# How far the expert stage runs ahead of the attention stage: a fixed lead in the merged order of an attention and expert-layer kernel

## The chip, the cores and the metric

The kernel runs on the 8 cores of one Trainium2 chip. Every core works on one sequence of 4096 tokens and writes its own output; nothing is exchanged between the cores. The metric is the device time of the slowest core in microseconds (us), lower is better.

## What is computed

For each sequence x (4096 tokens, 1024 numbers each) the reference does one linear-attention layer and one mixture-of-experts layer, each between two layer normalizations and with a residual:

```python
# attention: 8 heads of 64
q, k, v = x @ Wq, x @ Wk, x @ Wv
q = softmax(q, axis=-2) * SCALE        # over the 64 numbers of a head
k = softmax(k, axis=-1)                # over the 4096 tokens
context = einsum('bhdn,bhen->bhde', k, v)
out = einsum('bhde,bhdn->bhen', context, q) ... @ Wo + bo
# experts: 16 routed, top 2 by softmax score, and 2 shared
xe = einsum('bsd,eod->bseo', u, Wr) + br
routed = einsum('bse,bseo->bso', g_topk, xe)
shared = (einsum('bsd,eod->bso', u, Ws) + sum(bs)) / N_s
ffn = u + routed + shared
# the layer
x = x + layernorm(attn(layernorm(x)))
x = x + layernorm(ffn(layernorm(x)))
```

## The kernel before

The 4096 tokens are 32 tiles of 128. All 18 expert matrices are applied to every token, and the gate (zero for the experts that were not chosen) multiplies each product as it is added up, so the expert layer is a dense pass of 18 matrices of 1024 by 1024.

First comes a pass over all 32 tiles for keys and values (tags a1_...), which ends with the context. Everything behind it is one list, `flow_tail`. It has six windows, w = 0 to 5, and each merges two lists:

- `la`, the attention items of quarter w (8 tiles, taken in pairs, 21 items a tile, 168 items in all). For a tile: the query product (a2_p_q, L798), its exponential on ScalarE, the softmax division on VectorE (qn, L485 to L494), a transpose on TensorE (trqn, L811), the product with the context (o2, L823) and its copy (L509), the output product (wo, L840), bias and statistics (att, L518 to L526), normalization and residual (y, L530 to L539), the second normalization (ub, L545), its transpose (trub, L852), the scores (sc, L861), the gates on VectorE (g, L564 to L584, a chain of 12 small operations) and their transpose (trg, L870). Windows 4 and 5 have none.
- `lb`, the expert items: for w of 2 and more the final step of quarter w-2 (`fin_quarter`, 24 items: for each of 8 tiles statistics of the sum racc, the normalization L633 and the residual L636, with the residual loaded to yld and the result stored by DMA), then the expert pass of quarter w-1 (`ffn_quarter`, 644 items). That pass starts with s = 0: 16 groups of five matmuls (one of L879 and four of L884), which put the biases and u itself into racc through the copy L605. Then for s = 1 to 18 and both halves oh of the output (36 units) it loads a block of weights two units ahead (ffnl, 8 transposing DMAs, L400 to L404) and runs 8 groups, one a token tile: eight matmuls (ffnp, L895) and one multiply-and-add into racc on VectorE (ffnv, L610).

`prop_merge` (L275) writes the common order of a window: behind each item of `la` it puts items of `lb`, at the rate of `len(lb)/len(la)` times 0.65, so that about a third of `lb` is left over and stands at the window's end without attention items. Every engine takes its own items from the one list in that order, and each queue is executed strictly in order: TensorE (PE), VectorE (DVE), ScalarE (ACT) and the DMA queue of SyncE (SP), which holds all loads and stores of this part.

The products land in six PSUM banks (pb). They are given out while the list is read: each product takes the bank whose last reader stands furthest back in the list, and waits for that reader. The transposes have two banks of their own (pbT). The expert products of a quarter cannot be copied to racc before the final step of the quarter ahead has read racc (the wait at L602 for vFF of the same tile).

On SP a weight load ffnl waits until the unit that used the buffer has ended (L398), and the item a2_v_y (L374) stores the attention result and loads the rows of x and of the normalized input for two tiles later (L377 to L391).

Of the kernel before, what the change touches and what calls it, by code (L numbers as in the profile page):

```python
# [85 lines left out]
def build_nc():  # L86
# [185 lines left out]
        its.append(("finb", q, QT - 1))  # L272
        return its

    def prop_merge(la, lb):  # L275
        outl = []
        na, nb = len(la), len(lb)
        if na == 0:
            return list(lb)
        ratio = nb / na  # L280
        ib = 0
        for ia in range(na):
            outl.append(la[ia])
            want = int(round((ia + 1) * ratio * 0.65))
            while ib < want:
                outl.append(lb[ib]); ib += 1
        outl.extend(lb[ib:])
        return outl
# [4 lines left out]
    for w in range(NQ + 2):  # L293
        la = []
        if w < NQ:
            for t in range(QT * w, QT * w + QT, 2):
                la += zip_merge(a2_items(t), a2_items(t + 1))
        lb = []
        if 2 <= w:
            lb += fin_quarter(w - 2)  # L300
        if 1 <= w <= NQ:
            lb += ffn_quarter(w - 1)
        flow_tail += prop_merge(la, lb)
# [776 lines left out]
```

How the kernel before makes its waits and increments, by code:

```python
    def ms(self, eng, chan, label):  # L61
        self._bump(chan, label, 1)
        if self.mode == "emit":
            eng.drain().then_inc(self.sem[chan], 1)
# [1 line left out]
    def pe_ms(self, instr, chan, label):  # L66
        self._bump(chan, label, 1)
        if self.mode == "emit":
            instr.then_inc(self.sem[chan], 1)
# [1 line left out]
    def op_ms(self, instr, chan, label):  # L71
        self._bump(chan, label, 1)
        if self.mode == "emit":
            instr.then_inc(self.sem[chan], 1)
# [1 line left out]
    def dma(self, eng, chan, label, out, in_, **kw):  # L76
        self._bump(chan, label, 16)
        if self.mode == "emit":
            eng.dma_start(out=out, in_=in_, **kw).then_inc(self.sem[chan], 16)
# [1 line left out]
    def wait(self, eng, chan, label):  # L81
        if self.mode == "emit":
            eng.wait_ge(self.sem[chan], self.vals[chan][label])
```

## Times and profile before

| | us |
|---|---|
| time, median of 2 runs | 3333.73 (3290.99 and 3376.48) |
| profiled execution, its own time | 3106.46 |
| its span (slowest core, core 1) | 3104.8 |
| spans of the 8 cores | 3079.2 to 3104.8 |
| PE matmul busy | 2449.4 (79%) |
| DVE busy | 1578.0 (51%) |
| ACT busy | 113.7 (4%) |

The profiled execution is one run of the program; its own time stands below both timed runs. A row of the timeline shows when an instruction or a merged run of equal ones starts, how long it lasts, the engine and line, the operation and, in brackets, how long the engine had been idle before it and what ended that. "DVEq" is the queue of VectorE, that is a semaphore that VectorE sets when its work has drained.

### The profile page before, as it was taken

To read this page: it belongs to the slowest core of one execution; us is meant where nothing else is said; L and a number is where in the kernel's file an instruction comes from. 1 tells how busy PE (TensorE), PEld (TensorE's weight loads), DVE (VectorE), ACT (ScalarE), POOL (GpSimd) and SP (SyncE) were. 2 spreads that over 40 slices of the span, in tenths; PEclk is the share of its full clock that TensorE was granted. 3 is DMA by queue.
4 is the path that set the end of the run, shared out by engine and by line. 5 is a ranking of instruction groups with operands and counts; after the bars stand their busy time and mean duration, and the time that the engine had idled before them with its cause. 6 is when DMAs were issued, how large, how long until landed. Compare 5 with 4: busy or idle time off the path is not lost.

```text
span 3104.8 us, 38462 instructions; the slowest of 8 cores (3079.2 to 3104.8 us)
## 1 busy us (share of the span) xinstructions
PE 2449.4 (79%) x12014; PEld 1109.0 (36%) x12014; DVE 1578.0 (51%) x2882; ACT 113.7 (4%) x353; POOL 15.8 (1%) x29
## 2 busy tenths in 40 slices
PE   3243350349999999499999994999999949999994
PEld 1121120114444444234444442444444414444442
DVE  4132332666656644566566445666564454444445
ACT  0000000000000000000000000000000000000000
POOL 0000000000000000000000000000000000000000
PEclk9666675669999999799999996999999979999997
DMA  5989889213334433424344334243434342333334
GB/s 109 136 123 131 153 125 136 80 60 75 72 87 101 102 76 75 142 77 96 67 102 102 78 75 144 74 98 66 101 82 80 75 143 55 80 75 77 78 75 133
DMA packets 678005, 296.33 MB, mean 95 GB/s; under 512 B 632337, under 2 KB 643089, under 8 KB 676660
## 3 DMA queue, kind: packets, MB, share of 16 engines
q1 hardware_dynamic: 672628, 251.86, 34.0%
q0 software_dynamic: 5184, 42.01, 11.9%
q8 instruction: 107, 1.75, 0.2%
q14 instruction: 86, 0.70, 0.1%
HBM read 142.78 MB, written 79.69 MB: 72 GB/s over the span
## 4 chain that ended last, share of the span: by engine, by line
PE 65%; DVE 11%; DMA 7%; DVEq 6%; issue 4%; another core or an unknown queue 3%; SPq 3%; ACT 0%; POOL 0%; ACTq 0%; POOLq 0%
PE pb L895 56%; DMA xA<-xin 6%; SPq L79 2%; DVEq L424 2%; PE pb L840 2%; PE pb L798 2%; PE pb L884 2%; DVE att L535 1%; DVEq L64 1%; DVE ftmp L636 1%; DMA cen_st<-cen 1%; DVEq L532 1%; PE pb L754 1%; DVE Dbn L422 1%
## 5 line engine op out<-in xcount | busy, mean ns | idle before, releaser
L895 PE MATMUL pb<-wrt,uT 128*128 128x512 bf16 x9216 | 2019.7, 380 | 1.1 <-issue 0.3
L895 PEld LDWEIGHTS pb<-wrt,uT 128*128 128x128 bf16 x9216 | 895.5, 98 | 1072.7 <-issue 11.2
L610 DVE SCALAR_TENSOR_TENSOR racc<-pb,gAll,racc 128x512 f32<-128x512 f32 x1024 | 758.4, 750 | 836.1 <-PE pb L895 811.3
L740 PE MATMUL pbT<-eye,hb 128*128 128x128 bf16 x256 | 32.1, 306 | 236.0 <-DVEq L64 235.6
L610 DVE SCALAR_TENSOR_TENSOR racc<-pb,halfc,racc 128x512 f32<-128x512 f32 x128 | 96.1, 751 | 124.9 <-PE pb L895 124.9
L852 PE MATMUL pbT<-eye,ub 128*128 128x128 bf16 x256 | 23.1, 243 | 138.0 <-DVEq L64 137.7
L740 PEld LDWEIGHTS pbT<-eye,hb 128*128 128x128 bf16 x256 | 24.8, 138 | 242.1 <-issue 241.9
L422 DVE BATCH_NORM_STATS2 Abn<-xA 128x6 f32<-128x512 f32 x32 | 22.2, 693 | 154.2 <-DMA xA<-xin 150.8
L461 DVE CAST vb<-pb 128x512 bf16<-128x512 f32 x32 | 22.2, 694 | 107.9 <-PE pb L767 82.9
L884 PE MATMUL pb<-eyeblk,uT 128*128 128x512 bf16 x256 | 77.0, 430 | 0.0
L811 PE MATMUL pbT<-eye,qn 128*128 128x128 bf16 x128 | 13.5, 233 | 78.6 <-DVEq L64 78.2
L852 PEld LDWEIGHTS pbT<-eye,ub 128*128 128x128 bf16 x256 | 18.4, 109 | 149.1 <-issue 146.5
L535 DVE TENSOR_TENSOR att<-att,xA 128x1024 f32<-128x1024 f32 x32 | 39.2, 1226 | 62.0 <-DMA xA<-xin 55.5
L840 PE MATMUL pb<-wob,o2b 128*128 128x512 bf16 x256 | 66.6, 410 | 1.9 <-DVEq L64 1.9
L754 PE MATMUL pb<-wkb,hT 128*128 128x512 bf16 x256 | 67.8, 431 | 0.0
L798 PE MATMUL pb<-wqb,hT 128*128 128x512 bf16 x240 | 62.7, 413 | 0.4 <-issue 0.2
L605 DVE COPY racc<-pb 128x512 f32<-128x512 f32 x64 | 42.5, 689 | 33.8 <-PE pb L884 29.3
L879 PE MATMUL pb<-brx,gTx 18*128 18x512 bf16 x64 | 27.4, 429 | 40.1 <-DVE racc L605 40.1
L767 PE MATMUL pb<-wvb,hT 128*128 128x512 bf16 x256 | 56.6, 379 | 0.0
L721 ACT ACTIVATE Elv<-Eag,epsc 128x1 f32<-128x1 f32 x32 | 9.5, 297 | 1283.5 <-DVEq L64 1283.5
L494 DVE TENSOR_SCALAR qn<-qe,rq 128x64 bf16<-128x64 f32 x256 | 44.7, 250 | 4.6 <-issue 2.0
L633 DVE TENSOR_SCALAR ftmp<-racc,Eag,Ers 128x1024 f32<-128x1024 f32 x32 | 26.0, 812 | 41.0 <-DMA yld<-yscr 32.2
(109 smaller groups left out, 908.4 us busy)
## 6 DMA issues: line engine op xcount, KB each, us to landing
xA<-xin SPq DMA_DIRECT2D x128, 256.0 KB, 5.8
wbf<-wr POOLq DMA_DIRECT2D x16, 2048.0 KB, 39.8
wrt<-wbf SPq DMA_TRANSPOSE x1152, 2.8
yscr<-att SPq DMA_DIRECT2D x32, 512.0 KB, 3.5
yld<-yscr SPq DMA_DIRECT2D x32, 512.0 KB, 4.2
out<-ftmp SPq DMA_DIRECT2D x32, 512.0 KB, 2.9
hscr<-hT SPq DMA_DIRECT2D x32, 256.0 KB, 41.3
hT<-hscr SPq DMA_DIRECT2D x60, 128.0 KB, 4.6
```

Of the source, the lines that this page charges most:

```text
L79: eng.dma_start(out=out, in_=in_, **kw).then_inc(self.sem[chan], 16)
L422: v.bn_stats(bn[:, 0:6], src[:, 0:512])
L424: v.drain()
L535: v.tensor_tensor(att[i][:], att[i][:], xA[i][:], ALU.add)
L610: ii = v.scalar_tensor_tensor(rsl, pb[bk][:], gcol, rsl, ALU.mult, ALU.add)
L740: last = pe.transpose(pT[:, kk * P:(kk + 1) * P], hb4[i4][:, kk * P:(kk + 1) * P], eye[:])
L754: last = pe.matmul(pb[0 if i == 0 else 4][:], hT4[i4][:, kk * P:(kk + 1) * P], wkb[:, kk * HID:(kk + 1) * HID], start=(kk == 0), stop=(kk ...
L767: last = pe.matmul(pb[1 if i == 0 else 5][:], hT4[i4][:, kk * P:(kk + 1) * P], wvb[:, kk * HID:(kk + 1) * HID], start=(kk == 0), stop=(kk ...
L798: last = pe.matmul(pb[bk][:], hsrc[:, kk * P:(kk + 1) * P], wqb[:, kk * HID:(kk + 1) * HID], start=(kk == 0), stop=(kk == 7))
L840: last = pe.matmul(pb[bk][:], o2b[i][:, jx * P:(jx + 1) * P], wob[:, jx * D + oh * HID:jx * D + (oh + 1) * HID], start=(jx == 0), stop=(jx ...
L884: last = pe.matmul(pb[bk][:], uT[:, kk * NTOK + tt * P:kk * NTOK + (tt + 1) * P], eyeblk[:, kx * HID:(kx + 1) * HID], start=False, stop=(k ...
L895: last = pe.matmul(pb[bk][:], uT[:, kk * NTOK + tt * P:kk * NTOK + (tt + 1) * P], wrt[par][:, kk * HID:(kk + 1) * HID], start=(kk == 0), s ...
```

## The change

`prop_merge` gets a parameter `lead` with the value 36. The first 36 items of `lb` are now put ahead of the first item of `la`, and the rest of `lb` is spread by its own rate, `(len(lb) - 36)/len(la)` times 0.65. Window 0 has no `lb`, and windows 4 and 5 no `la`, so that their lists stay as they were. In window 1 (`lb` of 644) the 36 items are the 32 of s = 0, one weight load, one full group and the product of the next. In windows 2 and 3 (`lb` of 668) they are the 24 items of the final step and 6 groups of s = 0. The rate behind them goes from 2.49 to 2.35 items of `lb` for an attention item in window 1, and from 2.58 to 2.45 in windows 2 and 3.

```diff
-    def prop_merge(la, lb):
+    def prop_merge(la, lb, lead=36):
         outl = []
         na, nb = len(la), len(lb)
         if na == 0:
             return list(lb)
-        ratio = nb / na
-        ib = 0
+        lead0 = min(lead, nb)
+        ib = lead0
+        outl.extend(lb[:ib])
+        ratio = (nb - lead0) / na
         for ia in range(na):
             outl.append(la[ia])
-            want = int(round((ia + 1) * ratio * 0.65))
+            want = min(nb, lead0 + int(round((ia + 1) * ratio * 0.65)))
             while ib < want:
                 outl.append(lb[ib]); ib += 1
         outl.extend(lb[ib:])
```

The changed file is two lines longer, so its line numbers behind this place are higher by 2: L895 there is L897.

**Place 1: TensorE at the start of window 2.** Before, the two query products (L798) come first, then the two transposes of qn (L811), and only then the first groups of s = 0 (L879 and L884) with the products of the context (L823) between them:

```order
L895 MATMUL pb<-wrt,uT 128x512 x912
L798 MATMUL pb<-wqb,hT 128x512 x16
L811 MATMUL pbT<-eye,qn 128x128 x8
L879 MATMUL pb<-brx,gTx 128x512
L884 MATMUL pb<-eyeblk,uT 128x512 x4
L823 MATMUL pb<-qTt,ctx 64x128 x8
```

Now six groups of s = 0 stand ahead of the first query product; these rows are the sixth of them and what follows:

```order
L881 MATMUL pb<-brx,gTx 128x512
L886 MATMUL pb<-eyeblk,uT 128x512 x4
L800 MATMUL pb<-wqb,hT 128x512 x8
L881 MATMUL pb<-brx,gTx 128x512
L886 MATMUL pb<-eyeblk,uT 128x512 x4
L800 MATMUL pb<-wqb,hT 128x512 x8
```

The query products moved behind six groups, and eight groups now stand between the first query product and the first transpose of qn.

**Place 2: VectorE at the start of window 2.** Before, the softmax division of the first two tiles (L485, L489, L494) stands inside the final step (statistics L422 to L425, results L633 and L636):

```order
L422 BN_STATS Ebn<-racc 128x6
L423 BN_STATS Ebn<-racc 128x6
L425 BN_AGGR Eag<-Ebn 128x2
L485 TENSOR_REDUCE qs<-qe 128x8
L489 RECIPROCAL rq<-qs 128x8
L494 TENSOR_SCALAR qn<-qe,rq 128x64 x8
L633 TENSOR_SCALAR ftmp_58<-racc,Eag,Ers 128x1024
L636 TENSOR_TENSOR ftmp_58<-ftmp_58,yld_56 128x1024
```

Now the final step runs through, and the division stands behind eleven copies of s = 0 (L607):

```order
L635 TENSOR_SCALAR ftmp_59<-racc,Eag,Ers 128x1024
L638 TENSOR_TENSOR ftmp_59<-ftmp_59,yld_57 128x1024
L607 COPY racc<-pb 128x512 x11
L487 TENSOR_REDUCE qs<-qe 128x8
L491 RECIPROCAL rq<-qs 128x8
L496 TENSOR_SCALAR qn<-qe,rq 128x64 x8
L607 COPY racc<-pb 128x512
```

The attention work left the final step; the final step is now as it always was in window 4.

**Place 3: TensorE in window 1, the last pair of tiles.** Before, 104 matmuls (13 groups) of the expert pass stand between the second output product (L840) and the first transpose of ub (L852):

```order
L840 MATMUL pb<-wob,o2b 128x512 x8
L895 MATMUL pb<-wrt,uT 128x512 x104
L852 MATMUL pbT<-eye,ub 128x128 x8
L895 MATMUL pb<-wrt,uT 128x512 x8
L852 MATMUL pbT<-eye,ub 128x128 x8
```

Now it is 96 (12 groups), and at the pair's end the two transposes of the gates have no group between them (x2):

```order
L842 MATMUL pb<-wob,o2b 128x512 x8
L897 MATMUL pb<-wrt,uT 128x512 x96
L854 MATMUL pbT<-eye,ub 128x128 x8
L897 MATMUL pb<-wrt,uT 128x512 x8
L854 MATMUL pbT<-eye,ub 128x128 x8
L897 MATMUL pb<-wrt,uT 128x512 x32
L863 MATMUL pb<-ct_bf,uT 128x16 x8
L897 MATMUL pb<-wrt,uT 128x512 x8
L863 MATMUL pb<-ct_bf,uT 128x16 x8
L897 MATMUL pb<-wrt,uT 128x512 x64
L872 MATMUL pbT<-eye,gb 16x128 x2
```

One group moved out of the stretch to the window's end. Over the four pairs this stretch had 14, 12, 13 and 13 groups in window 1 and has 13, 12, 12 and 12; in windows 2 and 3 it had 13, 13, 13 and 14 each and has 13 four times.

## Rows read from the trace of the kernel before

**Rows 1.** Page: busy tenths of PE and its granted clock in 40 slices.
```profile
PE   3243350349999999499999994999999949999994
PEclk9666675669999999799999996999999979999997
```
**Rows 2.** Waits of PE from 680 us: total us, times, longest us.
```profile
PE pbT L811 <- DVEq L64: 60.1, 6, 22.1
PE pb L879 <- DVE racc L605: 40.1, 1, 40.1
PE pbT L852 <- DVEq L64: 28.3, 13, 3.9
PE pb L823 <- DVEq L64: 21.8, 2, 11.1
PE pbT L870 <- DVEq L64: 12.9, 13, 1.8
```
**Rows 3.** Timeline of PE, start of window 2.
```profile
1224.67 43.33 PE L895 MATMUL pb<-wrt,uT 128*128 128x512 bf16 x200
1267.84 3.62 PE L798 MATMUL pb<-wqb,hT 128*128 128x512 bf16 x16
1293.36 0.59 PE L811 MATMUL pbT<-eye,qn 128*128 128x128 bf16 x4 [21.91 <-DVEq L64]
...
1320.05 0.60 PE L879 MATMUL pb<-brx,gTx 18*128 18x512 bf16 x1
...
1322.40 0.38 PE L879 MATMUL pb<-brx,gTx 18*128 18x512 bf16 x1
```
**Rows 4.** Timeline of PE, start of window 4.
```profile
2505.42 0.38 PE L879 MATMUL pb<-brx,gTx 18*128 18x512 bf16 x1
...
2553.33 0.58 PE L879 MATMUL pb<-brx,gTx 18*128 18x512 bf16 x1 [40.13 <-DVE racc L605]
...
2558.02 0.38 PE L879 MATMUL pb<-brx,gTx 18*128 18x512 bf16 x1
...
2559.30 0.39 PE L879 MATMUL pb<-brx,gTx 18*128 18x512 bf16 x1
```
**Rows 5.** Timeline of VectorE, final step in window 2.
```profile
1282.15 0.81 DVE L633 TENSOR_SCALAR ftmp<-racc,Eag,Ers 128x1024 f32<-128x1024 f32 x1 [9.68 <-DMA yld<-yscr]
...
1319.55 1.89 DVE L605 COPY racc<-pb 128x512 f32<-128x512 f32 x3 [0.26 <-DVEq L64]
```
**Rows 6.** Timeline of VectorE, final step in window 4.
```profile
2521.53 0.81 DVE L633 TENSOR_SCALAR ftmp<-racc,Eag,Ers 128x1024 f32<-128x1024 f32 x1 [11.22 <-DMA yld<-yscr]
...
2552.50 3.68 DVE L605 COPY racc<-pb 128x512 f32<-128x512 f32 x6 [0.26 <-DVEq L64]
```
**Rows 7.** Timeline of PE, window 1: gaps ahead of three kinds of transposes.
```profile
699.18 0.38 PE L811 MATMUL pbT<-eye,qn 128*128 128x128 bf16 x4 [1.96 <-DVEq L64]
...
799.24 0.38 PE L811 MATMUL pbT<-eye,qn 128*128 128x128 bf16 x4 [1.29 <-DVEq L64]
...
845.91 1.01 PE L852 MATMUL pbT<-eye,ub 128*128 128x128 bf16 x8 [3.94 <-DVEq L64]
...
948.75 0.61 PE L852 MATMUL pbT<-eye,ub 128*128 128x128 bf16 x8 [2.26 <-DVEq L64]
```
**Rows 8.** Timeline of PE, last pair of window 2.
```profile
1661.02 0.61 PE L852 MATMUL pbT<-eye,ub 128*128 128x128 bf16 x8 [1.09 <-DVEq L64]
```
**Rows 9.** Timeline of VectorE, window 1 ahead of ub of the second pair.
```profile
831.02 2.07 DVE L610 SCALAR_TENSOR_TENSOR racc<-pb,gAll,racc 128x512 f32<-128x512 f32 x3 [0.26 <-issue]
...
842.18 2.73 DVE L610 SCALAR_TENSOR_TENSOR racc<-pb,gAll,racc 128x512 f32<-128x512 f32 x4 [0.26 <-PE pb L895]
```
**Rows 10.** Timeline of SP's DMA queue, window 1, first pair.
```profile
728.23 24.04 SPq L79 DMA_TRANSPOSE wrt<-wbf  x16
...
757.32 1.21 SPq L79 DMA_DIRECT2D hT<-hscr  x2
```
**Rows 11.** Page: time from issue to landing (last number) of the loads of hT.
```profile
hT<-hscr SPq DMA_DIRECT2D x60, 128.0 KB, 4.6
```

## The prediction

> **What bounds the kernel now.** I read the page's slices first. From the tenth slice on TensorE is at nine tenths or more, apart from a dip at each of the slices 17, 25 and 33 and at the end, and in those dips the granted clock falls to about 0.6 or 0.7 [rows 1]. So behind the first two windows (where nothing changes) the time is TensorE's own work plus its gaps. That work is the same before and after: the change only reorders. A group of the expert pass (eight matmuls of 512 columns) takes 1.73 us: 25 groups fill 1224.67 to 1267.84 [rows 3].
>
> The waits of TensorE from 680 us say which gaps exist [rows 2]. All end at VectorE: transposes of qn (L811) 60.1 us in 6 waits, the context product (L823) 21.8 in 2, transposes of ub (L852) 28.3 in 13, transposes of the gates (L870) 12.9 in 13, and one wait of 40.1 us of the s = 0 groups (L879). That is 163 us. The timeline of TensorE splits them. The long ones are the starts of windows 2, 3 and 4, where the final step of a quarter keeps VectorE; the short ones recur in each pair of attention tiles. The window starts are what a lead could help, and the short gaps are what a lower rate of expert groups could harm.
>
> **Window starts, before.** In window 2 the last expert group ends at 1267.84 and TensorE is back in steady work at 1320.05 [rows 3], 52.2 us. Inside it did the two query products (2 x 1.73, as they are eight such matmuls each), two transposes and two context products (some 1.2 together at full clock, my estimate from a duration of 0.6 at the low clock for the transposes [rows 3], halved) and three groups of s = 0. A group of s = 0 takes 1.28 at full clock, 2558.02 to 2559.30 [rows 4]. So 8.5 us of the 52.2 were work and 43.7 were lost. The next group still runs at the low clock, 2.35 instead of 1.28 [rows 3], which makes 44.8.
>
> **Window starts, after.** Six groups of s = 0 come first. They fill the six banks, and the query product behind them needs a bank whose copy VectorE makes only after the final step. So the lead does not put TensorE 18 groups ahead here: it goes six groups and stops. This is exactly what window 4 does already: its seventh group waits 40.1 us [rows 4]. What remains is when VectorE gets through. Residual rows land 14.3 us after the last group (1267.84 to 1282.15 [rows 3, 5]), behind the last weight loads on SP's queue, which the change leaves where they are. From there to the first copy the final step takes 31.0 us when it runs through, 2521.53 to 2552.50 [rows 6]; with the attention items between it took 37.4, 1282.15 to 1319.55 [rows 5]. TensorE resumes 0.8 after the first copy starts [rows 4, 6]. 14.3 + 31.0 + 0.8 = 46.1, less six groups of work (7.7) is 38.4 lost. The clock is low afterwards: the first two groups take 4.7 (2553.33 to 2558.02) for 2.6 of work [rows 4], 2.1 more. That is 40.5 against 44.8: **4.3 us less in each of windows 2 and 3, 8.6 together.** If the residual rows land as in window 4 (16.1 after the last group, 2505.42 to 2521.53 [rows 4, 6]) it is 2.5 each, 5.0 together.
>
> Here the Trainium skill speaks against the change: Perfetto Trace Analysis, section Optimization Strategy, says that where a kernel has several regimes with different busiest engines, interleaving them may improve it, and the lead takes the attention items out of the final step. The trace has both forms, and the interleaved one is not better here, since both regimes want VectorE (37.4 us against 31.0 [rows 5, 6]). By the rule the sum's first term would be a loss; what it would cost is in the second rival.
>
> **What leaves the final step's cover.** The softmax divisions of the first pair (half of 37.4 - 31.0, some 3 us a tile) now stand behind the final step, between groups of s = 0. Window 1 had this arrangement before, and TensorE waited 1.96 us for the second transpose of qn [rows 7]. I charge the same to windows 2 and 3, 3.9, and take off 0.7 in window 1, whose first pair now stands among the longer expert groups as its second pair does, with a gap of 1.29 [rows 7]. **3.2 us more.** Its bounds are 0 (VectorE catches up during ten groups) and 12.8 (all 6.4 us exposed twice).
>
> **The lower rate.** Between the second output product and the first transpose of ub, VectorE runs without a pause (bias, statistics, residual, statistics, ub) and TensorE arrives first. The gap follows the number of expert groups in that stretch: 14 groups 1.09 [rows 8], 13 groups 2.26, 12 groups 3.94 [rows 7]. So a group less costs 1.2 to 1.7 there. VectorE's side gives the same from below: its add takes 0.69 when it is busy (three in 2.07, four in 2.73 [rows 9]), and 1.73 - 0.69 = 1.04. The order has three groups fewer in window 1 (14, 12, 13, 13 before, 13, 12, 12, 12 after) and one fewer in each of windows 2 and 3. Five groups at 1.25 are **6.2 us more**; bounds 5.2 and 8.5. The gates' transposes wait about 1 us a pair (12.9 in 13 [rows 2]), for the second tile's chain mostly; their group counts stay near what they were, but the last pair of window 1 loses the one group between its two transposes: **1 us more**, between 0 and 1.7.
>
> **Edits that cost nothing.** In window 1 the 16 groups of s = 0 move ahead of the query products. They need what is there, and TensorE does the same work. The weight loads keep their place relative to the expert groups that need them. The stores and loads of a2_v_y move past weight loads on SP. Before, in window 1, 16 of these took 24.0 us and the last hT load went out at 757.32 + 1.21 [rows 10]; with 4.6 to land [rows 11] it was there at 763, and no wait for hT stands among TensorE's waits [rows 2]. After, the shortest way from the end of the awaited unit to the query product is 17 groups, 29.4 us, against 12 us for its eight weight loads, some 6 for the two tiles' own transfers and 4.6 to land, 22.6. It stays covered by 7 us.
>
> **The sum.** -8.6 + 3.2 + 6.2 + 1.0 = +1.8 us. On the profiled execution (3106.5, of which 3104.8 is span) that is 3108. The median of the two timed runs is 3333.7, 227 us above the profiled execution of the same program, for which these rows have no cause. The terms are in VectorE's and TensorE's durations, so I add them as they are: 3335.5, written as 3336.
>
> **Rivals.**
> (1) The lead helps more than I charge. Speaking for it: the attention items now come when expert groups are there to cover them, and a VectorE that is less behind might also shorten the gaps inside pairs. Against: these gaps follow the group counts, and the counts fall. If all short gaps of the pairs went (28.3 + 12.9 + 3.3) with the 8.6, that would be -53 us: 3053 on the profiled scale, 1.7% faster. A third of it is already generous.
> (2) The lost interleave costs, slower. The place is the first pair of windows 2 and 3, and then every pair's stretch ahead of ub. If the 6.4 us of attention work on VectorE are exposed in both windows (12.8), the residual lands late enough to take the gain, and each of 12 pairs waits the 3.94 of a 12-group stretch (47.3 instead of 28.3, 19 more), it is +32: 3138, 1.0% slower. It decides from where VectorE is still behind when the first transpose of qn comes.
> (3) SP becomes late, slower. If a weight load takes the place of the hT load and this lands 7 us after TensorE wants it at each of nine pairs, +63 us: 3169, 2.0% slower. It decides when the 22.6 us above exceed 29.4; weight loads would have to take 2.4 us each, and 16 of them in 24.0 us [rows 10] are 1.5 each.
> (4) The lead does nothing, because the banks stop TensorE after six groups and the rates differ by too little: 3106.
>
> **How the numbers follow.** My forecast, within 10 us of no change, has 0.6; rival 1 0.13, rival 2 0.17, rival 3 0.03, rival 4 0.07. On the scale of the timed median the first, second and third rivals end at 3281, 3366 and 3397; the forecast's own range is 3326 to 3346. What widens it is not the change: three executions of one program are at 3106, 3291 and 3376, and the changed kernel's median can fall at any of these levels. The range must hold them: 3100, near the profiled level, to 3400, the upper run and rival 2's cost less a little. About 2% is what a measurement of this kernel can tell from no change; no case but the third reaches it by itself, so most of the outer chances is this scatter: 0.06 faster, 0.87 the same, 0.07 slower.
>
> **What would show it.** Right: at the start of windows 2 and 3 six groups of s = 0, then one wait of TensorE of 38 to 41 us in place of several (the first of them 21.9 before [rows 3]); a final step of 31 us; the L852 waits at 33 to 37 us in total instead of 28.3, and near 4 us in the last three pairs of window 1. Wrong: a query product that waits for hT; weight loads that TensorE waits for; L852 waits that fall; or a window start whose wait is much shorter than window 4's.

## The result and the profile after

The changed kernel takes 3104.4 us (median of 30 runs), the kernel before 3119.3 in the same rounds (29 runs). Some runs of either kernel are disturbed and take some per cent more, as the two that gave 3334 us before did; the ratio of the undisturbed ones is 0.9946, 95% interval 0.9923 to 0.997, so 0.5% faster, some 17 us. I had forecast 1.8 us more, and my 3336 us stood on the median of those two runs.

The slices of the page (of the slowest core, here core 6) answer to [rows 1]; the dips at the starts of windows 2, 3 and 4 are still there.

```profile
PE   3243450359999899499999994999999949999994
PEclk9666675669999999799999997999999979999997
```

TensorE's waits after the change, core 1, from 680 us (line, what ended the wait: us in total, times, longest), answer to [rows 2]:

```profile
PE pb L800 <- DVE racc L607: 77.3, 2, 38.7
PE pb L881 <- DVE racc L607: 39.2, 1, 39.2
PE pbT L854 <- DVEq L64: 17.0, 8, 4.2
PE pbT L872 <- DVEq L64: 14.6, 13, 3.0
PE pbT L813 <- DVEq L64: 5.4, 5, 1.5
PE pb L897 <- DMA wrt<-wbf: 2.4, 2, 2.0
PE pb L897 <- DVE racc L612: 1.0, 1, 1.0
```

The window starts are one wait each, of the query product (L800) for a bank that the copy L607 frees. The surprise is L854, the transposes of ub: 17.0 us in 8 waits where there were 28.3 in 13, and where I had expected some 34.

TensorE's timeline at the start of window 2, after the change, answers to [rows 3]:

```profile
1246.18 0.39 PE L881 MATMUL pb<-brx,gTx 18*128 18x512 bf16 x1
...
1292.63 3.57 PE L800 MATMUL pb<-wqb,hT 128*128 128x512 bf16 x8 [38.66 <-DVE racc L607]
...
1298.04 1.89 PE L800 MATMUL pb<-wqb,hT 128*128 128x512 bf16 x8
...
1311.98 0.38 PE L813 MATMUL pbT<-eye,qn 128*128 128x128 bf16 x4 [1.54 <-DVEq L64]
```

To account for the whole, two landmarks on core 1: the last gate transpose of window 0 and the first s = 0 group of window 4. After the change:

```profile
661.32 0.27 PE L872 MATMUL pbT<-eye,gb 128*16 128x128 bf16 x1 [2.89 <-DVEq L64]
...
2473.83 0.38 PE L881 MATMUL pb<-brx,gTx 18*128 18x512 bf16 x1
```

That is 1812.5 us. Before, it was from 679.22 to 2505.42 [rows 4]:

```profile
679.22 0.26 PE L870 MATMUL pbT<-eye,gb 128*16 128x128 bf16 x1 [2.89 <-DVEq L64]
```

which is 1826.2, so 13.7 us fewer. The terms, each against its forecast:

| term | forecast | measured on core 1 |
|---|---|---|
| starts of windows 2 and 3 | -8.6 | -9.6 |
| transposes of qn | +3.2 | +2.1 (3.3 to 5.4) |
| transposes of ub | +6.2 | -11.3 (28.3 to 17.0) |
| transposes of the gates | +1.0 | +1.7 (12.9 to 14.6) |
| waits for weights and for a bank | 0 | +3.4 (2.4 and 1.0) |
| sum | +1.8 | -13.7 |

The start of window 2 went from 44.8 to 41.1 us lost: 46.45 from 1246.18 to 1292.63 less six groups (7.7), and 2.4 for the low clock up to 1298.04 (5.4 us for 3.0 of work). In window 3, worked the same way, it went from 46.2 to 40.3. So one term, the ub waits, carries the error: it is 17.5 us off, and the other four together 2.0 the other way.

The residual rows landed 14.6 us after the last expert group in window 2, and the final step then ran through in 31.0 us (1260.78 to 1291.79), as forecast. VectorE's timeline, answers to [rows 5] and [rows 6]:

```profile
1260.78 0.81 DVE L635 TENSOR_SCALAR ftmp<-racc,Eag,Ers 128x1024 f32<-128x1024 f32 x1 [10.06 <-DMA yld<-yscr]
...
1291.79 3.68 DVE L607 COPY racc<-pb 128x512 f32<-128x512 f32 x6 [0.26 <-DVEq L64]
```

The measure used below is the stretch from the last gate transpose of window 0 to TensorE's return in window 4, as the median of the eight cores: 1877.4 us before, 1861.6 after. It leaves out the pass for keys and values and window 0, which the change does not touch (the prediction's "first two windows"; window 1 does change): that part ended at 679.22 us in the one execution and at 661.32 in the other, so the time of a single execution cannot show terms of a few us. The stretch has a scatter too: two executions of one kernel (rate 0.80, below) differ by 5 us in it. Beside it stands the sum of the ub waits on core 1, which is nearly the same on every core (27.8 to 28.6 before, 16.8 to 17.2 after).

### The profile page after: what moved, and what is told of

The parts are those of the page before. It is cut to its first block, busy times and chain, and to the rows that moved or that the text cites. A ratio compares the mean times of both kernels' runs of the same rounds, so it can differ in the third digit from the quotient of the medians.

```text
span 3087.9 us, 38229 instructions; the slowest of 8 cores (3059.3 to 3087.9 us)
## 1 busy us (share of the span) xinstructions
PE 2432.7 (79%) x11781; PEld 1108.5 (36%) x12014; DVE 1577.1 (51%) x2882; ACT 113.0 (4%) x353; POOL 15.8 (1%) x29
## 4 chain that ended last, share of the span: by engine, by line
PE 65%; DVE 10%; DMA 8%; DVEq 5%; issue 4%; SPq 4%; another core or an unknown queue 3%; ACT 0%; POOL 0%; ACTq 0%; POOLq 0%
PE pb L897 56%; DMA xA<-xin 6%; SPq L79 4%; PE pb L842 2%; PE pb L800 2%; DVEq L426 1%; PE pb L886 1%; DVEq L64 1%; DVE ftmp L638 1%; DMA yld<-yscr 1%; DMA cen_st<-cen 1%; DVE att L537 1%; DVE ftmp L635 1%; PE pb L756 1%
## 5 line engine op out<-in xcount | busy, mean ns | idle before, releaser
L897 PE MATMUL pb<-wrt,uT 128*128 128x512 bf16 x9022 | 2011.9, 380 | 15.1 <-DMA wrt<-wbf 2.7
L897 PEld LDWEIGHTS pb<-wrt,uT 128*128 128x128 bf16 x9216 | 895.1, 98 | 1076.9 <-issue 18.2
L800 PE MATMUL pb<-wqb,hT 128*128 128x512 bf16 x230 | 63.1, 419 | 80.6 <-DVE racc L607 79.3
L854 PE MATMUL pbT<-eye,ub 128*128 128x128 bf16 x256 | 24.2, 251 | 124.8 <-DVEq L64 124.5
L424 DVE BATCH_NORM_STATS2 Abn<-xA 128x6 f32<-128x512 f32 x32 | 22.2, 693 | 146.7 <-DMA xA<-xin 143.7
L463 DVE CAST vb<-pb 128x512 bf16<-128x512 f32 x32 | 22.2, 694 | 108.2 <-PE pb L769 83.2
L886 PE MATMUL pb<-eyeblk,uT 128*128 128x512 bf16 x251 | 69.4, 400 | 0.7 <-issue 0.6
L854 PEld LDWEIGHTS pbT<-eye,ub 128*128 128x128 bf16 x256 | 19.4, 113 | 137.3 <-issue 135.7
L800 PEld LDWEIGHTS pb<-wqb,hT 128*128 128x128 bf16 x240 | 24.9, 105 | 113.7 <-issue 90.9
L607 DVE COPY racc<-pb 128x512 f32<-128x512 f32 x64 | 42.4, 688 | 34.2 <-PE pb L886 31.8
## 6 DMA issues: line engine op xcount, KB each, us to landing
wbf<-wr POOLq DMA_DIRECT2D x16, 2048.0 KB, 38.7
```

Of the source, the lines that this page charges most:

```text
L800: last = pe.matmul(pb[bk][:], hsrc[:, kk * P:(kk + 1) * P], wqb[:, kk * HID:(kk + 1) * HID], start=(kk == 0), stop=(kk == 7))
L886: last = pe.matmul(pb[bk][:], uT[:, kk * NTOK + tt * P:kk * NTOK + (tt + 1) * P], eyeblk[:, kx * HID:(kx + 1) * HID], start=False, stop=(k ...
L897: last = pe.matmul(pb[bk][:], uT[:, kk * NTOK + tt * P:kk * NTOK + (tt + 1) * P], wrt[par][:, kk * HID:(kk + 1) * HID], start=(kk == 0), s ...
```

## Experiments

The change has two parts, the lead and the lower rate behind it. The first three runs take them apart. Each kernel in this section but the last two was executed once, so a stretch below is that of one execution.

**The lower rate without the lead.**

```diff
-        ratio = nb / na
+        ratio = (nb - min(36, nb)) / na
         ib = 0
```

> The lower rate of the change (36 items of lb less in the rate) without the lead. Measured by the stretch from the last gate transpose of window 0 to TensorE's return in window 4, median of the 8 cores: 1877.4 us before, 1861.6 after the change; and by the sum of the waits ahead of the transposes of ub in windows 1 to 3: 28.3 before, 17.0 after. Rate theory (the prediction's step: a group less between wo and trub costs 1.25 us): stretch 1882 to 1886, ub waits 33 to 36. Cover theory (formed from the two traces: the wait follows the full expert groups between the first bias addition, att, and the first transpose of ub: 13 give 0 to 1, 12 about 2.2, 11 about 4, groups of s = 0 count less): these counts barely change without the lead, so ub waits 25 to 29, and the stretch 1873 to 1879. Both: the window starts stay at their three waits (about 78 us in windows 2 and 3 together).

Waits of TensorE in this kernel, core 1:

```profile
PE pbT L813 <- DVEq L64: 62.6, 8, 23.2
...
PE pb L825 <- DVEq L64: 22.7, 2, 11.5
PE pbT L854 <- DVEq L64: 17.4, 11, 3.9
PE pbT L872 <- DVEq L64: 16.6, 14, 1.8
PE pb L897 <- DVE racc L607: 3.6, 2, 1.8
```

The window starts stay about as they were (L813 and L825, 85.3 us in total against 81.9). But the ub waits fall to 17.4 with the lower rate alone: the step of my prediction has the wrong sign, and my second idea, a mere count of groups from att to the transpose, misses it too (25 to 29 expected). The stretch is 1874.0, inside what the second idea gave and only 3.4 us shorter, which is within the scatter of 5 us. On core 1 it is even 2.8 us longer (1876.9 against 1874.1): the 10.9 us come back as gate waits (3.7 more), waits for a bank (3.6), for weights (3.1) and in the L813 and L825 waits (3.4).

**The lead with the old rate.**

```diff
+        lead0 = min(36, nb)
+        ib = lead0
+        outl.extend(lb[:ib])
         ratio = nb / na
-            want = int(round((ia + 1) * ratio * 0.65))
+            want = min(nb, lead0 + int(round((ia + 1) * ratio * 0.65)))
```

> The lead of 36 with the rate of before. Rate theory: with the groups back in place the ub waits fall under those after the change, 17.0 to about 11, and the stretch is 1854 to 1857. Cover theory: counts between att and trub are 12, 11, 12, 12 in window 1 and 13, 12, 12, 13 in windows 2 and 3, so window 1 is no better than after the change: ub waits 17 to 21, stretch 1860 to 1866.

```profile
PE pb L800 <- DVE racc L607: 79.1, 2, 40.3
...
PE pbT L854 <- DVEq L64: 28.8, 14, 4.3
...
PE pbT L813 <- DVEq L64: 5.1, 6, 1.5
```

Both expectations miss: ub waits 28.8, as before the change, and stretch 1871.4. So the lead does nothing for the ub waits. The stretch is 6.0 us shorter, near the 5.4 that I had forecast for the starts and the qn waits together; that it comes from the window starts alone is likely, as they have the form that they have in the change (79.1 us in 2 waits), but with the scatter of 5 us it is not shown.

**The change in windows 2 and 3 only** (lead0 is 0 and the rate nb/na in window 1).

> The change in windows 2 and 3 only; window 1 keeps its old order. Windows 2 and 3 gained 12 of the 15.8 us by the traces and window 1 3.8. Cover theory: stretch 1863 to 1867, ub waits about 19.7 (10.5 in window 1 as before, 4.4 and 4.8 in windows 2 and 3). If the gain of windows 2 and 3 came from a better phase handed on by window 1, it would be 1870 or more.

```profile
PE pbT L854 <- DVEq L64: 19.8, 9, 3.9
```

Ub waits 19.8, as expected: 10.5 in window 1, as before, and 4.4 and 4.9 in windows 2 and 3. So the ub waits of windows 2 and 3 fall without the change in window 1. The stretch is 1867.0, at the end of the expected range and nearer to 1870 than the scatter can tell apart; the waits decide here, not the stretch.

**What a ub wait consists of.** The third pair of window 1 has 13 groups between the second output product and the transpose before the change and 12 after it, but in the merged order 12 between the first bias addition (att) and the transpose in both. It shows what a count leaves out. TensorE before, from the second output product (L840) to the transpose:

```profile
922.16 1.89 PE L840 MATMUL pb<-wob,o2b 128*128 128x512 bf16 x8
923.88 22.61 PE L895 MATMUL pb<-wrt,uT 128*128 128x512 bf16 x104
948.75 0.61 PE L852 MATMUL pbT<-eye,ub 128*128 128x128 bf16 x8 [2.26 <-DVEq L64]
```

VectorE before, at the start of its chain (L518 is the first bias addition, L610 the expert add ahead of it):

```profile
925.95 0.75 DVE L610 SCALAR_TENSOR_TENSOR racc<-pb,gAll,racc 128x512 f32<-128x512 f32 x1 [2.70 <-PE pb L895]
926.62 0.68 DVE L518 TENSOR_TENSOR att<-pb,boRep 128x512 f32<-128x512 f32 x1
```

TensorE after:

```profile
913.83 1.89 PE L842 MATMUL pb<-wob,o2b 128*128 128x512 bf16 x8
915.56 20.88 PE L897 MATMUL pb<-wrt,uT 128*128 128x512 bf16 x96
937.53 0.61 PE L854 MATMUL pbT<-eye,ub 128*128 128x128 bf16 x8 [1.08 <-DVEq L64]
```

VectorE after:

```profile
914.17 0.75 DVE L612 SCALAR_TENSOR_TENSOR racc<-pb,gAll,racc 128x512 f32<-128x512 f32 x1 [2.70 <-PE pb L897]
914.84 0.68 DVE L520 TENSOR_TENSOR att<-pb,boRep 128x512 f32<-128x512 f32 x1
```

Before, VectorE's queue has one more expert add ahead of the bias addition, and that add waits for the first of TensorE's 13 groups. So the chain starts 2.7 us after the second output product ended (926.62 against 923.88). After, it starts 0.7 us ahead of that end (914.84 against 915.56). The chain itself is about as long, 22.1 and 22.7 us from the bias addition to the transpose. TensorE gets to the transpose 19.9 us after the chain's start before and 21.6 after. That is 1.7 us more, the length of the output product, which now lies inside the chain, while the groups inside are 12 in both; the chain is 0.6 us longer, and the wait 2.26 - 1.08 = 1.2 us shorter, though the stretch has a group fewer. A group that VectorE must first wait for is no cover: it delays the chain by as much as it occupies TensorE.

The other pairs say the same. These are the waits of 80 of the 84 pairs of windows 1 to 3 on core 1 in seven kernels (before, after, the three above, and rate 0.66 and lead 28 below), by the groups that I had counted and by when the chain starts. The first pairs of windows 2 and 3 in the two kernels without a lead are left out, as most of their groups are the shorter ones of s = 0:

| groups from output product to transpose | chain starts 1.6 us or more after the output product's end | chain starts before its end |
|---|---|---|
| 14 | 0.9 to 1.1 us (6 pairs) | none |
| 13 | 2.1 to 3.2 (44 pairs), 0.9 (1) | 0 to 0.4 (10), 1.0 and 1.4 (2) |
| 12 | 3.6 to 4.3 (10) | 1.0 to 1.6 (7) |

Down each column a group fewer costs 1 to 2 us; from one column to the other it is 2 to 3 us at the same count.

From the pairs of the first kernels I put this in numbers. The chain is 16.7 us plus 0.69 for each expert add inside it; TensorE has 1.73 for each group that it runs from the release of the chain to the transpose, and about 1.2 more where the second output product falls inside. The difference, where positive, is the wait. These counts depend on the rounding in `prop_merge`, down to whether an attention item falls between a product and its add.

**A higher rate, 0.80 in place of 0.65, with the lead.** The edit is `ratio = (nb - lead0) / na * 80/65`.

> The change with 0.80 in place of 0.65, so that each stretch between att and trub has 14 or 15 expert groups. Cover theory: every ub wait goes (under 2 us in total instead of 17.0), the gate waits fall a little (14 to about 10), and the stretch is 1838 to 1846, if TensorE does not start to wait for weights or for hT. Rate theory expects the same sign: two groups more in 12 pairs at 1.25 each, but no more than the 17.0 that are there. A third possibility: the ub waits are VectorE's total work in a window and move elsewhere (waits of the expert products for racc or banks grow by as much), stretch 1858 to 1863.

```profile
PE pb L897 <- DMA wrt<-wbf: 9.1, 9, 1.7
PE pbT L872 <- DVEq L64: 5.8, 6, 1.2
PE pbT L813 <- DVEq L64: 3.2, 2, 1.7
```

No L854 wait for VectorE is left: the ub waits are gone, the gate waits fell from 14.6 to 5.8, and weights cost 9.1 instead of 2.4. The stretch is 1838.4, at the lower end of what was expected and 20 us under the third possibility. So the waits don't just move elsewhere on VectorE.

**The rate at 0.66, the lead as in the change.** This run asks whether it is the rate or the rounding:

```diff
-        ratio = (nb - lead0) / na
+        ratio = (nb - lead0) / na * 66/65
```

> The change with 0.66 in place of 0.65: the rate rises by 1.5%, so groups come back into the attention stretches. Chain theory (formed after the first four runs): the wait ahead of ub is VectorE's chain from the moment att may start to ub, 16.7 us plus 0.69 for each expert add in it, less 1.73 for each group TensorE has from that moment to the transpose, and about 1.2 less where the second output product falls inside. The order then gives single waits of 1.0, 3.9, 2.2, 2.2 and eight of 2.2: a sum of 27 us, against 17 at 0.65, and a stretch of 1869 to 1873 against 1861.6. Rate theories of either sign (more groups help, or fewer groups help) expect a change of under 1 us for 1.5%: sum 16 to 18, stretch 1860 to 1863.

```profile
PE pbT L854 <- DVEq L64: 28.6, 12, 4.3
PE pbT L872 <- DVEq L64: 11.0, 11, 1.4
```

1.5% more rate brings the ub waits from 17.0 back to 28.6. The chain theory said 27 and single waits of 1.0, 3.9, 2.2 and 2.2 in window 1; the timeline has 1.06, 4.30, 2.22 and 2.57, and eight waits of 2.22 to 2.57 in windows 2 and 3. The stretch, 1867.4, is 6 us above the change's and short of the 1869 to 1873 expected: gate, qn, weight and bank waits are together 8 us smaller than after the change on this core (15.3 against 23.4), so the other waits took back a part of what the ub waits cost.

**A lead of 28 in place of 36.**

> The change with a lead of 28 in place of 36 (24 of the final step and 2 groups of s = 0 in windows 2 and 3). Chain theory: the order gives 3.2 and 3.9 three times in window 1, and 2.2 in each pair of windows 2 and 3: ub waits 32 us in total. The window starts stay one wait on a softmax chain or bank, within 3 us of the change's; so the stretch is 1873 to 1880. A theory that the lead itself shortens the ub waits expects something between 17 and 28, on the way from no lead to 36, and a stretch between 1862 and 1872.

```profile
PE pb L881 <- DVE racc L607: 114.2, 3, 39.3
PE pbT L854 <- DVEq L64: 34.6, 12, 3.9
```

Ub waits 34.6 (32 expected by the chain theory, 17 to 28 by the other), stretch 1881.7, a little above the expected 1873 to 1880 and 20 us above the change's. That is also 4.3 above the kernel before any change, which is within the scatter, but the ub waits are longer than there (28.3) as well. A lead somewhat shorter is not somewhat less good; it falls on another rounding.

| kernel | ub waits, by the rule of the chain | measured, core 1 | stretch |
|---|---|---|---|
| before | 28.8 | 28.3 | 1877.4 |
| after | 16.8 | 17.0 | 1861.6 |
| lower rate alone | 22.2 | 17.4 | 1874.0 |
| lead at the old rate | 23.6 | 28.8 | 1871.4 |
| change in windows 2 and 3 | 18.2 | 19.8 | 1867.0 |
| rate 0.66 | 26.8 | 28.6 | 1867.4 |
| lead 28 | 32.4 | 34.6 | 1881.7 |
| rate 0.80 | 0.8 | 0 | 1838.4 |

Only the two rows of rate 0.66 and lead 28 were worked out before the run. The rule is off by 5 us in the two kernels with one part of the change: it treats the first pair of windows 2 and 3 too simply. With the lower rate alone these waited 0.8 each where it gives 4.0; with the lead at the old rate they waited 1.4 and 1.0 where it gives none, and the last pairs 2.1 in two waits where it gives 1.1.

**Two versions meant to beat both, timed.** The first is rate 0.80 again.

> The same kernel as lead36_r80 (0.80 in place of 0.65), timed. Its stretch was 39 us shorter than before's in one look, so 3081 to 3090 against about 3117 for the kernel before, a ratio of 0.985 to 0.990.

The ratio to the kernel before is 0.9878, interval 0.982 to 0.9936, and its stretch 1833.2. The ratio is as expected, about twice the gain of the change. The intervals of the two just touch (0.9923 is the change's lower end), but three of the four runs took 3064 to 3073 us, below all 30 of the change (lowest 3080.8).

The second moves the final step. In `ffn_quarter`:

```diff
-        for s in range(1, NSTEP):
+        for s in range(1, NSTEP - 1):
...
+        s = NSTEP - 1
+        for j in range(QT):
+            for oh in range(2):
+                its.append(("ffnp", q, s, oh, j))
+                its.append(("ffnv", q, s, oh, j))
+            its.append(("fina", q, j))
+            its.append(("finact", q, j))
+            if j >= 1:
+                its.append(("finb", q, j - 1))
+        its.append(("finb", q, QT - 1))
...
-        if 2 <= w:
-            lb += fin_quarter(w - 2)
```

The weight loads of the last two units stand behind this loop.

> An attempt to beat both: rate 0.80, lead 36, and the final step no longer stands at a window's start. The last matrix (both halves) of a quarter runs tile by tile, and each tile's final step follows its two groups, so that VectorE normalizes one tile while TensorE works on the next; the weight loads for the next quarter go out behind it. VectorE then needs some 42 us (16 adds and the final step's 31) beside 28 us of TensorE's work, so each of the three waits of 38 to 41 us at a window's start should become about 15, and the 39 us behind the last expert group at the kernel's end about 15 too: 90 us less than lead36_r80, a ratio to the kernel before of 0.955 to 0.965. If TensorE then waits for the late weight loads of the next quarter (24 us for 16), 30 us of it are lost and the ratio is 0.965 to 0.975.

Its waits, core 1 (line numbers are 12 higher):

```profile
PE pb L909 <- DMA wrt<-wbf: 54.1, 14, 11.9
PE pb L893 <- DVE racc L624: 15.0, 9, 2.4
PE pb L893 <- DVE racc L619: 12.3, 3, 5.5
```

TensorE's timeline at the end of the first quarter:

```profile
1206.35 25.16 PE L909 MATMUL pb<-wrt,uT 128*128 128x512 bf16 x104 [10.03 <-DMA wrt<-wbf]
...
1237.59 0.37 PE L893 MATMUL pb<-brx,gTx 18*128 18x512 bf16 x1 [2.15 <-DVE racc L624]
...
1257.62 0.58 PE L893 MATMUL pb<-brx,gTx 18*128 18x512 bf16 x1 [3.39 <-DVE racc L619]
```

The ratio is 0.9697, interval 0.9532 to 0.9862. The wait of about 39 us at a window's start is gone; in its place stand 10 us for weights and some 9 us in small waits for VectorE. A third part is in the granted clock. TensorE's clock through these waits (columns: stretch, its length, PE busy, PEld, DVE, ACT, POOL, granted clock, DMA share, GB/s):

```profile
1260.00:1265.00 5.00, 5.00 (x12) 1.10 (x11) 1.85 (x4) 0.00 (x0) 0.00 (x0) 0.50 0.50 105
```

It is 0.50 from about 1240 to 1265 us, where a group of s = 0 takes 2.35 us in place of 1.28, and for some 5 us after the wait for weights. From the end of the group ahead of that wait (1196.32) to 1266.63, where TensorE is back at full clock, it is 70.3 us for 38.8 of work (15 expert groups and 10 of s = 0). Of the 31.6 lost, 19.3 are the waits and about 12 the low clock; I had expected about 15 in all. The kernel's end, from the last matmul on, fell from 39.7 us (rate 0.80) to 23.8, where I had also expected 15. The forecast of 0.955 to 0.965 lies within the interval of the ratio, so it is by these parts that it was too good, not by the ratio. The wait for weights has a reason in the order that I had not seen: running both halves of the last matrix tile by tile needs the second half's weights one unit (13.8 us) sooner than before. A wait of this size (9.9 to 11.9 us on core 1) stands near the end of each of the four quarters. The other loss I had named, late weights of the next quarter, does not show in the timeline: TensorE goes from the s = 0 groups into the expert groups there without a wait.

## Why the prediction was wrong

The first steps held. The lead puts TensorE six groups ahead in windows 2 and 3 and no more, as the banks allow: one wait of 38.7 us (38 to 41 forecast). The starts were forecast at -8.6 us and gave -9.6. The final step took the 31.0 us that it was given, and taking the attention items out of it did not cost, against the rule on interleaving. The qn waits (+3.2 forecast, +2.1) and the gates (+1.0, +1.7) were right in sign and near in size. The lead alone, 5.4 us forecast for starts and qn waits, gave 6.0; so close a match is partly luck, given the scatter of 5.

The step that failed is the lower rate: "Five groups at 1.25 are 6.2 us more". Measured is -11.3, and the run with the lower rate alone (17.4 against 28.3) shows that this term has the other sign by itself. I had counted the groups between the second output product and the transpose, and read a price from three waits that fell in a row (14, 13, 12 groups: 1.09, 2.26, 3.94). The price was about right for pairs of that kind (the left column of the table of pairs); what failed is that I took the kind as fixed. In all three pairs the chain started 2.7 us after the output product ended. A group whose add stands ahead of the bias addition in VectorE's in-order queue delays the chain, and a lower rate takes such groups away too. With the rounding as it fell the second output product now lies inside the chain in six of twelve pairs of the changed order, against two before, and there a pair waits 2 to 3 us less at the same count. The run at 0.66 shows how little of this is the rate: a rate 1.5% higher undoes it.

The edit I cost at nothing had a small price, 2.4 us for weights on core 1 and up to 7.6 on core 0. The first rival came nearest: it named gaps that shrink although counts fall, and I gave it 0.13 and called a third of its 53 us generous; the measured 13.7 to 17 us are about that third. Its reason, a VectorE that is less behind, is not what the runs show. What stays open is how the last few us add up: the rate alone gives -3.4 and the lead alone -6.0, the two together -15.8, but two executions of one kernel (rate 0.80) differ by 5 us in the stretch, so the missing 6 may be scatter. The ub waits nearly add up (-10.9 for the rate, +0.5 for the lead, -11.3 together).

## What to carry to other kernels

Where two streams of work are merged into one order for in-order queues, a wait is the second engine's chain, from the moment its first item can start, less what the first engine does from that same moment. Count work from there, not from the last product of the chain on the first engine: work that the chain's engine has to wait for ahead of its first item is delay, not cover. And before believing in a merge constant, shift it by one or two per cent; here 0.65 to 0.66 moved the ub waits by 12 us, while real steps gave more: 0.80 gave 1.2%, and 0.80 with the final step moved beside the last matrix 3% (1.4% to 4.7%).

## What the runs showed of the chip beyond that

A ub wait of about 2.2 us costs more than itself in some cases, because the clock falls. TensorE's timeline of the run at rate 0.66, core 1, where the clock fell at the wait:

```profile
1355.05 1.01 PE L854 MATMUL pbT<-eye,ub 128*128 128x128 bf16 x8 [2.22 <-DVEq L64]
1355.86 3.09 PE L897 MATMUL pb<-wrt,uT 128*128 128x512 bf16 x8
1358.79 0.61 PE L854 MATMUL pbT<-eye,ub 128*128 128x128 bf16 x8
```

And its clock in two stretches of 2 us from there (PE busy, PEld, DVE, ACT, POOL, granted clock, DMA share, GB/s):

```profile
1355.00:1357.00 2.00, 1.95 (x11) 1.28 (x12) 1.72 (x3) 0.00 (x0) 0.00 (x0) 0.50 0.96 312
...
1359.00:1361.00 2.00, 2.00 (x17) 1.06 (x14) 0.75 (x1) 0.00 (x0) 0.00 (x0) 1.00 1.02 345
```

The changed kernel, same wait and no fall:

```profile
1451.77 0.61 PE L854 MATMUL pbT<-eye,ub 128*128 128x128 bf16 x8 [2.22 <-DVEq L64]
1452.22 1.89 PE L897 MATMUL pb<-wrt,uT 128*128 128x512 bf16 x8
1453.94 0.61 PE L854 MATMUL pbT<-eye,ub 128*128 128x128 bf16 x8
```

From the first to the second transpose it is 3.74 us in the one and 2.17 in the other: the granted clock was 0.50, the lower of the two levels (1.2 GHz), for some 3 us, and that cost 1.6 us on top of the 2.22. After the same idle time of 2.22 us the clock fell in the one case and not in the other; no run here shows what decides it. A transpose of ub takes 0.61 us at full clock. Over the eight cores (each has 24 of these transposes) those that took more than 0.65 were 24 before, 25 after, 22 with the lower rate alone, 34 with the lead at the old rate, 25 with the change in windows 2 and 3, 32 at rate 0.66, 47 at lead 28 and none at 0.80. So slow clocks at the ub waits have no part in the change's own gain. At lead 28 they are 23 more than before, some three a core, which by an estimate from the 1.6 us above is at most 4.6 us of what it lost.

The ub waits themselves repeat closely, within 0.8 us from core to core in a sum of 28. What varies is what hangs on DMA: waits for weights were 2.4 us on core 1 and 7.6 on core 0 of one execution. A term of a few us is better read from the waits of one trace than from times, where 29 and 30 runs still left an interval of half a per cent.
